# The down projection's weights and its first two tiles split and multiplied inside the gate-and-up stage

## What is computed

```python
def _sparsify_2to4(h):
    B, S, I = h.shape
    g = h.reshape(B, S, I // 4, 4)
    a = jnp.abs(g)
    _, idx = jax.lax.top_k(a, 2)
    pos = jnp.arange(4)
    mask = (pos == idx[..., 0:1]) | (pos == idx[..., 1:2])
    return (g * mask.astype(g.dtype)).reshape(B, S, I)
h = jax.nn.silu(jnp.einsum('bsh,hi->bsi', x, w_gate)) * jnp.einsum('bsh,hi->bsi', x, w_up)
h_sparse = _sparsify_2to4(h)
return jnp.einsum('bsi,ih->bsh', h_sparse, w_down)
...
x = x + jnp.tanh(g_ffn[0]) * _L0_ffn_ref(_layernorm(x, axis=-1), L0_ffn_w_gate, L0_ffn_w_up, L0_ffn_w_down)
```

## Time and profile before

| | |
|---|---|
| time, median of 3 runs (lowest, highest) | 2247.9 us (2247.34, 2250.03) |
| the profiled execution: its own time | 2249.69 us |
| its span in the trace | 2247.9 us |
| mean granted PE clock | 0.963 |
| PE, DVE, ACT, POOL busy share | 89%, 61%, 48%, 19% |
| gate_up, about | 1210 to 1627 us |
| down, about | 1627 to 1826 us |

### The profile page before, as it was taken

How to read it: one execution, slowest core, us unless ns; L and a number is a source line. 1 busy time by engine, 2 the same in 40 slices (tenths; PEclk the granted TensorE clock), 3 DMA queues, 4 the chain that set the end, 5 groups by cost and what they waited for, 6 DMA issues and landing times. The chain is left out here.

```text
span 2247.9 us, 33557 instructions
## 1 busy us (share of the span) xinstructions
PE 1996.2 (89%) x10802; PEld 1531.6 (68%) x10818; DVE 1371.1 (61%) x2400; ACT 1073.3 (48%) x2593; POOL 425.4 (19%) x504
## 2 busy tenths in 40 slices
PE   6999479999989999987997999999689979997898
PEld 5888357776767677766886778778578866665454
DVE  6777266666666666663323764554544328885786
ACT  3333156666656666653113412121134318885898
POOL 1111034444444444430000000000000001222110
PEclk9999789999999999998998999999899989998999
DMA  5665662323232321006443221112295322321111
GB/s 213 243 243 231 244 178 76 98 64 103 60 101 76 85 76 48 22 27 239 145 136 137 83 75 38 56 37 57 62 339 198 118 81 68 113 94 48 48 56 43
DMA packets 192217, 250.42 MB, mean 111 GB/s; under 512 B 11574, under 2 KB 143814, under 8 KB 181836
## 3 DMA queue, kind: packets, MB, share of 16 engines
q1 hardware_dynamic: 192076, 248.67, 33.9%
HBM read 152.14 MB, written 96.48 MB: 111 GB/s over the span
## 5 line engine op out<-in xcount | busy, mean ns | idle before, releaser
L930 ACT ACTIVATE at_prob<-at_S,at_bias,at_rq 128x384 f32<-128x384 f32 (+1 forms) x256 | 184.2, 731 | 165.3 <-DVE at_bias L1016 159.1
L1027 DVE TENSOR_TENSOR at_pt_lo<-at_PT,at_pt_hi 128x512 fp32r<-128x512 f32 x224 | 148.8, 688 | 92.6 <-ACT at_pt_hi L937 92.6
L798 POOL TENSOR_SCALAR at_prob<-at_prob,at_rsum 128x384 f32<-128x384 f32 (+1 forms) x256 | 160.3, 639 | 174.7 <-DVE at_rsum L1022 174.7
L1444 ACT ACTIVATE gu_silu<-gu_G 128x512 f32<-128x512 f32 x64 | 38.3, 598 | 269.6 <-PE gu_G L103 260.1
L857 PE MATMUL at_PT<-c_ident,at_prob 128*128 128x128 f32 x896 | 127.8, 277 | 44.1 <-DVE at_pt_lo L1027 44.1
L937 ACT ACTIVATE at_pt_hi<-at_PT 128x512 fp32r<-128x512 f32 x224 | 127.9, 604 | 53.1 <-PE at_PT L857 53.1
L1007 DVE TENSOR_REDUCE at_nmax<-at_S 128x1 f32<-128x384 f32 (+1 forms) x256 | 147.7, 615 | 4.7 <-PE at_S L850 4.2
L857 PEld LDWEIGHTS at_PT<-c_ident,at_prob 128*128 128x128 f32 x896 | 97.7, 140 | 75.6 <-DVE at_pt_lo L1027 71.2
L1477 DVE TENSOR_TENSOR gu_h<-gu_silu,gu_U 128x512 f32<-128x512 f32 x64 | 43.9, 687 | 154.6 <-PE gu_U L103 109.7
L846 PE MATMUL at_S<-at_k_hi,at_q_hi 128*128 128x384 f32 (+1 forms) x256 | 112.7, 440 | 16.6 <-DVE at_q_lo L1032 13.4
L789 POOL TENSOR_TENSOR at_rq<-at_qv,c_minus_half 128x4 f32<-128x4 f32 x64 | 65.1, 1017 | 288.0 <-DVE at_qv L1002 288.0
(11 more groups left out here) (272 smaller groups left out, 5658.5 us busy)
## 6 DMA issues: line engine op xcount, KB each, us to landing
wide<-at_ot SPq DMA_DIRECT2D x64, 256.0 KB, 2.9
wide<-gu_h SPq DMA_DIRECT2D x64, 256.0 KB, 3.2
o_a<-wide SPq DMA_DIRECT2D x14, 1024.0 KB, 4.8
d_a<-wide SPq DMA_DIRECT2D x14, 1024.0 KB, 4.8
keys_hi<-kv_kt_hi SPq DMA_DIRECT2D x8, 1024.0 KB, 4.0
keys_lo<-kv_kt_lo SPq DMA_DIRECT2D x8, 1024.0 KB, 6.0
values_hi<-kv_v_hi SPq DMA_DIRECT2D x8, 1024.0 KB, 8.0
values_lo<-kv_v_lo SPq DMA_DIRECT2D x8, 1024.0 KB, 9.6
```

Source lines behind the costliest of these rows:

```text
L798: pool.tensor_scalar(prob[u % 2][:, h, 0:n], prob[u % 2][:, h, 0:n], rsum[:, s:s + 1], 1.0, ALU.mult, ALU.mult).then_inc(normed.sem, 1)
L930: act.activation(prob[u % 2][:, h, 0:n], S[h][:, 0:n], ACT.Exp, bias=bias[:, s:s + 1], scale=rq[u % 4][:, h:h + 1], accum_out=sums[:, s:s ...
L1027: dve.tensor_tensor(pt_lo[f % 4][:], bank_of("p", u, kb)[:], pt_hi[f % 4][:].bitcast(F32), ALU.subtract).then_inc(pt_done.sem, 1)
```

## The change

Both sides of the border between gate_up and the second down projection change; nothing else does. The `o_` use of `down` keeps its code.

1. A new `make_down` allocates, before gate_up and until the end of down, the buffers `down_w_hi`, `down_w_lo`, `down_a_hi0/1`, `down_a_lo0/1` and two PSUM banks. In gate_up the same rooms hold six of the eight pairs of split gate and up weights, and two of the four banks for transposes.
2. In the last turn of gate_up, SP loads the four weight parts of w_down and tiles 0 and 1 of turn 0 (1 MB each, n = 0 to 5) into the buffers `x` and `xn`, which that turn does not need. ACT and DVE split piece n in step `SPLIT_AT` (4, 6, 8, 10, 13, 14), between the silu or product of that step and what followed it. After step 15 PE makes the 96 matmuls of tiles 0 and 1.
3. In down the loads and splits of weights, the split of tiles 0 and 1, their matmuls and the fillers are gone. Tile 2 is now the one that is loaded in quarters, PE starts it after `add(0)`, and the first two pieces of the last stage's weights are both loaded at tile 3.

```diff
+def three_terms(pe, Y, a_hi, a_lo, w_hi, w_lo, k):
+
+    pe.matmul(Y[:], a_hi[:, k, :], w_hi[:, k, :], start=(k == 0), stop=False)
+    pe.matmul(Y[:], a_lo[:, k, :], w_hi[:, k, :], start=False, stop=False)
+    return pe.matmul(Y[:], a_hi[:, k, :], w_lo[:, k, :], start=False, stop=(k == IC - 1))
...
@@ down @@
-            pe.wait_ge(weights.arrived[0], 16)
-            keep_awake(pe, Y[0], c, AWAKE)
-            for j in range(WP):
-                for r in range(2):
-                    pe.wait_ge(first_lo, 2 * j + r + 1)
-                    pe.wait_ge(weights.ready, j + 1)
...
+            if made:
+                pe.wait_ge(y_done, 1)
+                for j in range(WP):
+                    pe.wait_ge(first_lo, j + 1)
                     for k in range(4 * j, 4 * j + 4):
-                        last = product(r, k)
+                        last = product(0, k)
...
@@ gate_up @@
+        down_raw = [(x, ln.xn)[n % 2][:] for n in range(WQ)] + \
+            [raw_a[:].rearrange("p a (b q) -> p (a b) q", q=P) for raw_a in (x, ln.xn)]
...
+        SPLIT_AT = {4: 0, 6: 1, 8: 2, 10: 3, 13: 4, 14: 5}
+        ROOM_FREE = [4, 4, 8, 8, 12, 12]
...
+                if not more:
+                    sp.wait_ge(*ln.xn_ready.at(turn, TT))
+                    load_down(0)
+                    sp.wait_ge(*T_full.at(turn, DC))
+                    load_down(1)
...
                 for q in range(NC):
+                    if not more and q >= 1:
+                        for n in ((2, 3), (4, 5), ())[q - 1]:
+                            sp.wait_ge(down_ready, n - 1)
+                            load_down(n)
                     sp.wait_ge(*sparse.at(turn, SP * (q + 1)))
...
+            for r in range(2):
+                pe.wait_ge(down_ready, WQ + r + 1)
+                for k in range(IC):
+                    last = three_terms(pe, c.rooms[f"Y{r}"], c.rooms[f"a_hi{r}"], c.rooms[f"a_lo{r}"], c.rooms["w_hi"],
+                                       c.rooms["w_lo"], k)
+                last.then_inc(c.early, 1)
...
@@ ACT, step i @@
+                    if not more and i in SPLIT_AT:
+                        n = SPLIT_AT[i]
+                        act.wait_ge(down_arrived[n], 16)
+                        act.wait_ge(*U_full.at(turn, ROOM_FREE[n]))
+                        act.activation(down_hi[n], down_raw[n], ACT.Copy).then_inc(down_hi_ready, 1)
                     if i % 4 == 0 and i >= 4:
                         sizes(turn, i // 4 - 1)
...
@@ DVE, step i @@
+                    if not more and i in SPLIT_AT:
+                        n = SPLIT_AT[i]
+                        dve.wait_ge(down_hi_ready, n + 1)
+                        dve.tensor_tensor(down_lo[n], down_raw[n], down_hi[n].bitcast(F32),
+                                          ALU.subtract).then_inc(down_ready, 1)
```

More of the change, by code:

```diff
@@ L1115, in down, with product_done @@
         block = ctx.enter_context(nc.Block())
+        def product_done(g):
+            if made:
+                return (c.early, g + 1) if g < 2 else (Y_full, g - 1)
+            return Y_full, g + 1
         def coming(g, k=0):
-            n = g - AHEAD - k if prepare else -1
-            return [n] if prepare and 0 <= n < SIGNS else []
+            n = g - AHEAD - k if made else -1
+            return [n] if made and 0 <= n < SIGNS else []
         def piece(n):
-            return weights.raw[n % WP][:].rearrange("p k n -> p (k n)")
+            return raw[n % WP][:].rearrange("p k n -> p (k n)")
         @block.sync
@@ L1170, in _ @@
         def _(pe):
[L1171 to L1174, removed]
             def turn_signs(n, part):
@@ L1223, in keep_signs @@
                     last.then_inc(kept, 1)
+            if made:
+                act.wait_ge(*product_done(0))
             for j in range(WP):
                 own = slice(4 * j, 4 * j + 4)
-                for r in range(2):
+                for r in range(1 if made else 2):
                     act.wait_ge(first_arrived[WP * r + j], 16)
                     act.activation(a_hi[r][:, own, :], a[r][:, own, :], ACT.Copy).then_inc(first_hi, 1)
[L1230 to L1233, removed]
+                if not made:
+                    weights.split_hi(act, j)
+            for g in range(QUICK, N):
+                act.wait_ge(a_arrived[g % 2], 16 * ((g - QUICK) // 2 + 1))
+                act.wait_ge(*product_done(g - 2))
                 act.activation(a_hi[g % 2][:], a[g % 2][:], ACT.Copy).then_inc(hi_done, 1)
@@ L1254, in _ @@
                 own = slice(4 * j, 4 * j + 4)
-                for r in range(2):
-                    dve.wait_ge(first_hi, 2 * j + r + 1)
+                for r in range(1 if made else 2):
+                    dve.wait_ge(first_hi, (1 if made else 2) * j + r + 1)
                     dve.tensor_tensor(a_lo[r][:, own, :], a[r][:, own, :], a_hi[r][:, own, :].bitcast(F32),
                                       ALU.subtract).then_inc(first_lo, 1)
-                weights.split_lo(dve, j)
-            for g in range(2, N):
+                if not made:
+                    weights.split_lo(dve, j)
+                elif j == 0:
+                    add(0)
+            for g in range(QUICK, N):
                 add(g - 2)
-                dve.wait_ge(hi_done, g - 1)
+                dve.wait_ge(hi_done, g - QUICK + 1)
                 dve.tensor_tensor(a_lo[g % 2][:], a[g % 2][:], a_hi[g % 2][:].bitcast(F32),
@@ L1290, in gate_up @@
     with ExitStack() as ctx:
+        c.make_down(nc)
         mem = Alloc(ctx, nc, "gu_")
@@ L1316, in gate_up @@
         w_ready = mem.sem("w_ready")
+        down_arrived = [mem.sem(f"down_arrived{i}") for i in range(WQ + 2)]
+        down_hi_ready = mem.sem("down_hi_ready")
+        down_ready = mem.sem("down_ready")
         x_arrived = mem.counter("x_arrived", 16)
@@ L2341, in __init__, with make_down @@
         self.ones = mem.sb("ones", [P, P])
+    def make_down(self, nc):
+        self.down = ExitStack()
+        for name in ("w_hi", "w_lo"):
+            self.rooms[name] = self.down.enter_context(nc.sbuf_tensor("down_" + name, [P, IC, D], F32R))
+        for name in ("a_hi0", "a_lo0", "a_hi1", "a_lo1"):
+            self.rooms[name] = self.down.enter_context(nc.sbuf_tensor("down_" + name, [P, IC, P], F32R))
+        for name in ("Y0", "Y1"):
+            self.rooms[name] = self.down.enter_context(nc.psum_tensor("down_" + name, [P, 512], F32))
+        self.early = nc.alloc_semaphore("down_early")
     def make_last(self, nc):
```

112 lines of the change are left out of this document (77 added, 35 removed).

## The result

The changed kernel takes 2231.2 us (median of 5 runs, 2228.1 to 2235.8) against 2247.9 us (2245.2 to 2250.8) in the same number of runs of the kernel before. The ratio is 0.9927 with a 95% interval of 0.9912 to 0.9942: about 0.7% or 16 us faster, clear of no change, at a forecast of 2229.6 us.

A forecast was written before the change was run, and what follows sets the result against it. The prediction took PE, busy 89% of the span, as the bound. Tile 2 in full swing at 1642.9 + 2.6 = 1645.5 against 1663.85 is 18.3 us earlier: 2229.6 us from 2247.9, range 2223 to 2238.

The forecast's parts named there:

- Where the gain lies: Border of gate_up and down: all hangs on when PE, in full swing, begins tile 2, before at 1663.85 us.
- Pieces 2 to 5 wait behind the stores, ACT with them, and its silu behind it: Last turn of gate_up: loads land late, ACT and DVE wait, the last choose ends 8.0 us later, at 1628.7.
- Piece 2 lands at 1568.7 + 8.8: Last turn of gate_up, step 8: piece 2 lands 8.8 us behind the first store of q = 0, at 1577.5.
- PE waits 0.5 and 1.0 us in gate_up: Last turn: PE waits 0.5 us for step 9's silu, 1.0 for step 12's product; gate_up ends at 1610.2.
- The border takes 6.3 us: From the last choose's end to down's first DMA: 6.3 us for four stores and the barrier, down starting at 1635.1.
- Tile 2 starts 7.8 us after down's first DMA: Start of down: x lands after 7.05 us (6.2 to 9.25), its addition takes 0.75, tile 2 starts at 1642.9.
- 2.6 us for the lower clock: Start of tile 2: after some 11 us idle, about 12 matmuls at half clock cost 2.6 us, bounds 1.7 and 5.
- the splits hide fully: Rival, gate_up's last turn: loads land 2 us or more sooner, PE ends last, 22.0 us gained, up to 24.5; chance 0.12.
- loads slow down stores: Rival, gate_up's last turn: landings 3 us later, choose ends 6 us later, gain 12 us, 2236 us; chance 0.09.
- No change: Rival, gate_up's last turn: loads land 18 us behind the first store, eating the gain; within 4.5 us, chance 0.04.
- slower: Rival, gate_up's last turn: at 22 us to landing, 8 us more than before, 2256 us; chance 0.05.
- the prediction's estimate from it: By the 512 B rule, gate_up's stores are through in 2.9 us instead of 5, each load pair about 2.2 us sooner.

The follow-up runs named there:

- one load at a time: Changed kernel, with SP waiting for piece 2 to land before issuing piece 3, and for 4 before 5: 2227.9 us, ratio 0.9916.
- the five traces of this order: Changed kernel, run twice, and three variants with its loads, stores and splits up to down's first DMA: medians 2229.4 to 2243.3 us.
- the kernel with loads ahead: Changed kernel, with pieces 2 and 3 issued ahead of the stores of q = 0, 4 and 5 ahead of those of q = 1: 2224.7 us.

## Why the prediction was right

The forecast was a gain of 18.3 us; the stretch shows 16.1 and the medians 16.7. Its steps, in its own order:

- *Where the gain lies.* Right: what PE has won is idle time at the border; new waits of 2.2 us in gate_up were covered. From tile 2's full swing to the last matmul both kernels take 161.4 us, once the 2.6 us of the lower clock are taken off.
- *Pieces 2 to 5 wait behind the stores, ACT with them, and its silu behind it.* Right in its mechanism, shown by moving the loads (5.0 us sooner to down's first DMA) and by adding one (5.7 later). One term was too small. "Piece 2 lands at 1568.7 + 8.8" had the landing of a load with none behind it; it was 10.0, and 9.75 at piece 4, together 2.1 us later. The last choose ended 9.3 us late instead of 8.0, so some 0.8 us of that were made good by a walk that was too long elsewhere: with one load at a time, where the 8.8 is met, the choose ended 7.5 us late. Over the five traces of this order it ended 8.0 to 9.7 us late, so the 8.0 was at the edge of what such a kernel does.
- *PE waits 0.5 and 1.0 us in gate_up.* Measured 1.37 and 0.78 us; its gate_up ended 2.6 us late instead of 1.5, more than the 2 us that the forecast had given as its sign. This cost nothing, as the early matmuls still ended before the stores landed, at 1630.5 against a first DMA at 1633.85.
- *The border takes 6.3 us.* 6.4 us.
- *Tile 2 starts 7.8 us after down's first DMA.* It was 8.7: x landed at 7.9 us instead of 7.05, within the bounds of 6.2 to 9.25.
- *2.6 us for the lower clock.* 2.6 us, by 12 matmuls. In the other kernels without fillers it was 1.6 to 2.9 us, so that the figure was met so well is partly luck.

Together: 1.3 us of choose and 0.9 us of x make up the 2.2 us between 18.3 and 16.1.

The rivals. That the splits hide fully needed loads that pass slow stores; they don't, by the trace. What it priced has been shown by issuing them ahead: the sum was 22.0 us gained, and the stretch of the kernel with loads ahead is 22.1 us shorter. Down's first DMA comes where that sum had it, 112.5 us into the turn; that the total agrees as well is luck, as x came 0.9 us later and the lower clock cost 0.9 us less. That loads slow down stores came true in kind but not in size: the last store of q = 0, issued first to landed, took 6.7 us instead of 5.3, where the rival had 3 us more, and DVE's waits for stores grew from 12.0 to 13.7 us without moving the end. No change and slower needed landings at 18 and 22 us; they were at 10. The Trainium skill, page "DMA: Bandwidth & Descriptors", section Specifications, gives 512 B as the least that reaches the full rate; by the prediction's estimate from it piece 2 would have landed at about 6.6 us. No load behind four stores landed before 8.6 us in any run. But that estimate asked too much of the rate, as it set a bare transfer of 2.9 us against 5 us from issue to landing. By the packets, 1.05 MB take 3.7 us at the stores' 287 GB/s and 3.2 at the loads' 330: the trace disagrees with the page by 0.5 us a megabyte, and as stores and loads also differ in direction, no run shows what the 512 bytes alone cost.

## What to carry to other kernels

Work moved under another stage is fed by that stage's queue: a load issued behind slow stores lands when they are through, and if an in-order engine waits for it, everything written behind that wait is late too. Issue the load when its buffer comes free, ahead of the next stores, rather than at the next place in the loop. When a stall is taken away, ask at once what starts the next piece of work: here the order of two small loads was worth 3 us. And when a figure is read from one trace, look up how far the same figure moves in kernels that share the code: here that was 1 to 2 us, as much as some of the effects.

## What the runs showed of the hardware

A transfer of one queue lands later when another stands behind it, though packets go in the order of issue. A load of 1 MB behind four stores landed 8.6 to 9.1 us after the first store's issue with no load right behind it, and 8.9 to 10.5 us with one. The last of four stores of 256 KB, those of q = 0, landed after 5.3 us with no load behind it (five traces) and after 6.7 to 6.8 us with one or more (seven traces). The last packet of these stores had ended after 4.7 us in the kernel before (1573.21, issued from 1568.49) and after 4.9 in the changed one (1570.94, from 1566.04), so the packets themselves were hardly later. Why the landing is, stays open.

The fillers' worth depends on what else PE could do: ten took 4.6 us, with tile 2 due 8.7 us after down's first DMA, and saved 2.6 us at the lower clock for 0.8 us of delay (one trace each; the lower clock cost 1.6 to 2.9 us in the traces without fillers, by 8 to 14 matmuls at 0.43 us, and no run shows what sets the number); where tile 2 was due 5.8 us after that DMA, ten cost 2.3 us of delay for 1.3 saved, and five 0.5 for 0.4.
